# Two interleaved image streams, and the last pair's experts in two turns, in a fused early-fusion kernel on one Trainium2 core

## The reference

```python
scores = jnp.einsum('bnd,bmd->bnm', inputs, inputs) / jnp.sqrt(d_k)      # layer 0, attention
_, idx = jax.lax.top_k(weights, k); sel_idx = idx[:, :kk]                # k = 96, kk = 95
processed = jnp.zeros_like(x).at[batch_idx, sel_idx].set(y)              # layer 0, feed-forward
```

## Time and profile before

| | us |
|---|---|
| median of 3 runs | 513.05 (510.72 to 514.03) |
| the profiled execution | 511.42 |
| its span, first to last instruction | 509.6 |
| TensorE busy | 458.2 (90%) |
| VectorE busy | 344.3 (68%) |
| ScalarE busy | 315.6 (62%) |
| POOL busy | 235.7 (46%) |

### The profile page before, as it was taken

One profiled execution on the slowest core, in us unless ns is written; L12 is line 12 of the kernel. 1 busy time (PEld: TensorE's weight loads), 2 busy tenths in 40 slices (PEclk: granted clock), 3 DMA queues, 4 the chain that ended last, 5 costly groups with the idle time before them and its releaser, 6 DMA issues.

```text
span 509.6 us, 14274 instructions
## 1 busy us (share of the span) xinstructions
PE 458.2 (90%) x5771; PEld 360.2 (71%) x5771; DVE 344.3 (68%) x1151; ACT 315.6 (62%) x675; POOL 235.7 (46%) x266
## 2 busy tenths in 40 slices
PE   7887898989998999989998999889998999789985
PEld 3444577777877878767876787777876787667763
DVE  3588779757995599568975799568956795344220
ACT  2337475767767676787666866778568657463322
POOL 3347733674347634653457525772475246620010
PEclk9999999999999899999999999999999899899999
DMA  8350240023101320033002310132003200231000
GB/s 299 107 99 1 49 96 2 2 44 71 23 10 22 65 44 4 2 82 65 3 4 42 64 32 3 23 65 51 10 3 83 45 3 3 42 72 30 3 1 9
DMA packets 13969, 21.38 MB, mean 42 GB/s; under 512 B 5024, under 2 KB 6544, under 8 KB 13776
## 3 DMA queue, kind: packets, MB, share of 16 engines
q1 hardware_dynamic: 13904, 20.47, 17.3%
HBM read 5.07 MB, written 0.79 MB: 11 GB/s over the span
## 4 chain that ended last, share of the span: by engine, by line
PE 40%; DVE 31%; ACT 14%; POOL 8%; issue 6%; DMA 1%; POOLq 0%; ACTq 0%; DVEq 0%
PE bank L1083 30%; PE bank L1116 9%; DVE negm L695 5%; DVE q_sb L630 4%; DVE tb L630 4%; DVE ssq L646 3%; POOL qs L879 2%; DVE on L712 2%; ACT qT L904 2%; POOL q_sb L872 1%; DMA qM<-mT 1%; ACT qs L904 1%; ACT L1036 1%; ACT xf L915 1%; POOL rsA L806 1%
## 5 line engine op out<-in xcount | busy, mean ns | idle before, releaser
L837 POOL TENSOR_TENSOR q_sb<-q_sb,tb 128x1024 f32<-128x1024 f32 x24 | 57.2, 2385 | 94.5 <-DVE tb L630 94.5
L695 DVE TENSOR_REDUCE negm<-bank 128x2 f32<-128x384 f32 (+2 forms) x112 | 68.1, 608 | 39.3 <-PE bank L1083 38.8
L904 ACT ACTIVATE qT<-bank 128x512 fp32r<-128x512 f32 x96 | 52.4, 597 | 42.8 <-PE bank L1116 42.0
L1083 PE MATMUL bank<-kS,qM 128*128 128x224 f32 (+3 forms) x384 | 64.8, 285 | 7.7 <-issue 4.4
L1083 PEld LDWEIGHTS bank<-kS,qM 128*128 128x128 f32 x384 | 55.0, 194 | 21.8 <-issue 8.6
L879 POOL TENSOR_TENSOR qs<-q_sb,qs 128x1024 fp32r<-128x1024 f32 x24 | 56.7, 2362 | 27.9 <-ACT qs L904 27.7
L1083 PE MATMUL bank<-vx,p 128*64 128x65 f32 x1024 | 65.4, 223 | 0.0
L1036 ACT ACTIVATE p<-bank 128x512 f32<-128x512 f32 x96 | 54.7, 592 | 12.6 <-PE bank L1083 12.3
L1083 PEld LDWEIGHTS bank<-vx,p 128*64 128x64 f32 x1024 | 57.3, 138 | 0.0
L1083 PE MATMUL bank<-qT,kh 128*128 128x512 f32 (+1 forms) x128 | 51.7, 445 | 2.2 <-ACT p L1036 1.2
L1116 PE MATMUL bank<-ident_r,qs 128*128 128x128 f32 x384 | 44.8, 258 | 3.8 <-POOL qs L879 2.7
(11 more groups left out here) (177 smaller groups left out, 1025.4 us busy)
## 6 DMA issues: line engine op xcount, KB each, us to landing
qM<-qT SPq DMA_DIRECT2D x48, 256.0 KB, 3.2
qM<-qM SPq DMA_DIRECT2D x1, 1280.0 KB, 9.3
wts<-weights SPq DMA_DIRECT2D x1, 1059.0 KB, 5.9
p<-masks SPq DMA_DIRECT2D x1, 960.0 KB, 9.8
h<-txt SPq DMA_DIRECT2D x1, 672.0 KB, 7.1
img<-images SPq DMA_DIRECT2D x8, 72.0 KB, 2.2
q_sb<-wqkv SPq DMA_DIRECT2D x1, 576.0 KB, 8.0
p<-experts SPq DMA_DIRECT2D x1, 512.0 KB, 10.3
```

The source lines that it names most:

```text
L695: ve.tensor_reduce(dst, src, AX_X, ALU.max, negate=True).then_inc(s_vec, 1)
L837: return gp.tensor_tensor(a, a, b[:, :, ::-1], ALU.add)
L904: return ac.activation(dst, src, ACT.Copy)
L1083: return pe.matmul(dst, lhsT, rhs, start=start, stop=stop, skip_group_check=True)
```

## The change

1. **Two image streams.** "A" takes the even pairs, a new stream "O" the odd ones. Each has its own buffers and its own four semaphores. Pair 1's image stage runs in `BANK_S` and does not wait for pair 0's; from pair 2 on all lie in `BANK_A` again, and pair n waits for y of pair n-1.
2. **Tokens by image.** The tiles are transposed in the order 0, 2, 1, so that the 192 tokens of an item lie side by side. s01 is 2 matmuls of 192 columns in place of 8, s2 2 in place of 4, route 2 in place of 8, all but s2 with full output rows.
3. **The last pair's experts in two turns.** D has nine turns. The eighth is pair 7's tiles 0 and 1 and begins after wo1; the ninth is tile 2 alone, after wo2, in the two banks `BANK_Q`, so that h1 does not wait for the activation of h0.
4. **Experts' own storage.** `picks`, `hmT` and `xd` get buffers of their own; E6 and E9 no longer wait for D.
5. **New orders.** All five strings of `MERGE`, and `WARM` with 90 and 29 idle matmuls.

The order of TensorE's last steps is, before: wo1 V6 V7 V8 X4 X5 wo2, then D of pair 7 (xT logits oneT h0 h1 h2 h3 out). After: wo1 V6 V7 D7.xT V8 D7.logits X4 D7.oneT D7.h0 D7.h1 X5 D7.h2 D7.h3 wo2 D7.out, then the ninth turn's eight steps. VectorE does D7's ln before V6, the rest of it after V8; ScalarE does h0 and h1 of D7 before the copy of X5.

At the start TensorE does A0.rows cols tok, A1.rows cols tok, A0.xT1 s01 s2, A1.xT1, A0.ctx, A1.s01 s2 ctx, A0.xT2 route h1a, A1.xT2 route, A0.h1b y, A1.h1a h1b, and rows and cols of pair 2 around A1.y, then B. VectorE does rank1 and rank2 of pair 1 before y of pair 0, and rank3 of pair 1 before h of pair 0. ScalarE does xn1 of pair 1 before the second exponential of pair 0, xn2 and xT2 of pair 1 before h1a of pair 0. Before V0 stand E0, E1, E2 and S3; tok, xT1, s01, s2 and ctx of pair 2 stand ahead of E0.

The diff's core (the strings and the repeated indexing by pair left out):

```diff
-D_PE = ["y0", "y1", "y2", "xT", "logits", "oneT", "h0", "h1", "h2", "h3", "out"]
+D_PE = ["xT", "logits", "oneT", "h0", "h1", "h2", "h3", "out"]
...
+def turn(names, pair, name):
+
+    return pair.half * len(names) + names.index(name) + 1
...
            "A": [("A", x) for x in A_ORDER],
+           "O": [("A", x) for x in A_ORDER],
...
+PAIRS_OF = {"D": range(PAIRS + 1), "A": range(0, PAIRS, 2), "O": range(1, PAIRS, 2)}
...
+        xa, xpad = two("xa", [P, NT, D + 1]), two("xpad", [P, 2, D + 1])
+        xaT, h1T = two("xaT", [P, PT]), two("h1T", [P, 2, PT])
...
-        picks = small[:, 0:PT].rearrange("q (t c) -> q t c", t=NT)
+        picks = sb("picks", [P, NT, P])
-        hmT = early21[:, 0:4 * PT].rearrange("k (c q) -> k c q", c=4)
-        xd = small[:, 2 * PT:2 * PT + NT * D].rearrange("q (t d) -> q t d", t=NT)
+        hmT = sb("hmT", [P, 4, PT])
+        xd = sb("xd", [P, NT, D])
...
+        def d_tiles(p):
+
+            return (0, NT) if p.n < PAIRS - 1 else (0, 2) if p.n < PAIRS else (2, NT)
...
+        def d_bank(p, c=0):
+
+            return bank[BANK_D if p.n < PAIRS else BANK_Q[c % 2]]
+
+        def a_bank(p, name=None):
+
+            if p.n == 0 and name is not None:
+                return dict(s2=BANK_O, h1a=BANK_D, h1b=BANK_O, y=BANK_E[0])[name]
+            return BANK_S if p.n == 1 else BANK_A
...
-                    if n == 6:
-                        ac.wait_ge(d_pe, p.n * len(D_PE))
+                    if n in (6, 9) and p.n > 0:
+                        ac.wait_ge(o_pe, p.n * NV)
...
             def a_rows(p):
-                if p.n == 0:
+                if p.n < 2:
                     pe.wait_ge(ld_first, 16)
                 else:
-                    pe.wait_ge(a_vec, p.n * len(A_VEC))
+                    pe.wait_ge(a_vec[p.par], p.half * len(A_VEC))
+                if p.n > 2:
+                    pe.wait_ge(a_vec[1 - p.par], turn(A_VEC, Pair(0, p.n - 1), "y"))
...
-                    transposes(bA, [src[:, t, 0:D] for t in range(NT)], ident, a_pe)
+                    transposes(bank[a_bank(p)], [src[p.par][:, t, 0:D] for t in (0, 2, 1)], ident, a_pe[p.par])
...
                 for b in range(2):
-                    c0, c1 = cols(b)
-                    halves(bA[:, T * b:T * b + P], xaT[:, c0], xaT[:, c0], True, True)
-                    ins = halves(bA[:, T * b + P:T * b + T], xaT[:, c0], xaT[:, c1], True, True)
-                ins.then_inc(a_pe, 1)
+                    ins = mm(bank[a_bank(p)][:, image(b)], xaT[p.par][:, own(b)], xaT[p.par][:, image(b)], True, True)
+                ins.then_inc(a_pe[p.par], 1)
...
-                    pe.wait_ge(d_act, after(D_ACT, p, ["oneT", "h0", "h1", "h2"][c]))
+                    pe.wait_ge(d_act, after(D_ACT, p, ["oneT", "h0", "h1", "h2"][max(0, c - 1) if p.n == PAIRS else c]))
```

More of the change, by code:

```diff
@@ L407, in a_rows @@
                 if p.n + 2 < PAIRS:
-                    sp.wait_ge(a_pe, after(A_PE, p, "rows"))
+                    sp.wait_ge(a_pe[p.par], turn(A_PE, p, "rows"))
                     image(p.n + 2)
@@ L556, in _, with rt @@
             halves = [(slice(0, P), 0, 0, 0), (slice(0, P), 1, 1, 0), (slice(0, 64), 0, 2, 1), (slice(64, P), 1, 2, 1)]
-            before = cs("before").rearrange("q (k s) -> q k s", k=2)
-            rt = bA[:, 0:2 * T].rearrange("q (b t) -> q b t", b=2)
+            seen = cs("before").rearrange("q (k s) -> q k s", k=2)
+            before = [seen[:, :, HALF:HALF + T], seen[:, :, 0:T]]
+            def rt(p):
+                return bA(p)[:, 0:2 * T].rearrange("q (b t) -> q b t", b=2)
             def a_rank1(p):
-                ve.wait_ge(a_pe, after(A_PE, p, "route"))
-                if p.n == 0:
+                ve.wait_ge(a_pe[p.par], turn(A_PE, p, "route"))
+                if p.n < 2:
@@ L576, in a_rank2 @@
                                                   ALU.is_equal, ALU.mult)
-                ins.then_inc(a_vec, 1)
+                ins.then_inc(a_vec[p.par], 1)
             def a_rank3(p):
-                ve.wait_ge(a_vec, after(A_VEC, p, "equal"))
+                ve.wait_ge(a_vec[p.par], turn(A_VEC, p, "equal"))
                 for q, b, t, k in halves:
-                    ins = ve.scalar_tensor_tensor(eq[q, t, :], rt[q, b, :], wcol[q, t:t + 1], eq[q, t, :],
-                                                  ALU.is_gt, ALU.add, accum_out=rank[q, t:t + 1])
@@ L594, in a_y @@
[L594 to L596 removed]
+                ve.tensor_tensor(yA[p.par], bank[a_bank(p, "y")][:, 0:NT * D].rearrange("q (t d) -> q t d", t=NT),
+                                 wt("b2").unsqueeze(1).broadcast_to([P, NT, D]), ALU.add).then_inc(a_vec[p.par], 1)
+                ve.wait_ge(a_vec[p.par], turn(A_VEC, p, "y"))
@@ L604, in b_ln @@
+                ve.tensor_tensor(h0[:, p.n, :, :], hx[p.par][:, :, :], yA[p.par], ALU.add).then_inc(a_vec[p.par], 1)
             def b_ln(p):
-                ve.wait_ge(a_vec, after(A_VEC, p, "h"))
+                ve.wait_ge(a_vec[p.par], turn(A_VEC, p, "h"))
                 sums(h0[:, p.n, :, :], sumsB, b_vec)
@@ L743, in d_pick @@
                 wait_apart(ve, d_vec, after(D_VEC, p, "top"))
-                for t in range(NT):
+                for t in range(lo, hi):
                     ins = ve.max_index(ix[:, t, :], top[:, t, :], lg[:, t, :])
@@ L929, in d_xn @@
                 ac.wait_ge(d_pool, after(D_POOL, p, "shift"))
-                normalise(xd, hC, rsD, nmD, d_act)
+                for t in range(*d_tiles(p)):
+                    ins = ac.activation(xd[:, t, :], hC[:, t, :], ACT.Identity, scale=rsD[:, t:t + 1], bias=nmD[:, t:t + 1])
+                ins.then_inc(d_act, 1)
             def a_do(name, dst, src, func=ACT.Copy, **kw):
                 def f(p):
-                    if p.n == 0 and name[0] == "h1a":
+                    if p.n < 2 and name == "h1a":
                         ac.wait_ge(ld_w, 16)
-                    ac.wait_ge(a_pe, after(A_PE, p, name[0]))
-                    ac.activation(dst, src if src is not None else bank[a_bank(p, name[0])][:, 0:dst.shape[1]], func,
-                                  **kw).then_inc(a_act, 1)
+                    ac.wait_ge(a_pe[p.par], turn(A_PE, p, name))
+                    b = bank[a_bank(p, name if name in ("s2", "h1a", "h1b") else None)]
+                    ac.activation(dst[p.par], b[src[0], 0:src[1]], func, **kw).then_inc(a_act[p.par], 1)
                 return f
             def a_h1(c):
-                return a_do(["h1a", "h1b"][c:c + 1], h1T[:, c, :], None, ACT.Gelu_apprx_tanh,
+                return a_do(["h1a", "h1b"][c], [h[:, c, :] for h in h1T], (slice(0, P), PT), ACT.Gelu_apprx_tanh,
                             bias=wt("b1")[:, c:c + 1])
@@ L1148, in a_xt, with image, own @@
-                return f
-            def cols(b):
-                return slice(P * b, P * b + P), slice(2 * P + HALF * b, 2 * P + HALF * b + HALF)
+                    wait_apart(pe, a_act[p.par], turn(A_ACT, p, wait))
+                    transposes(bank[a_bank(p)], [src[p.par][:, t, 0:D] for t in (0, 2, 1)], ident, a_pe[p.par])
+                return f
+            def image(b):
+                return slice(T * b, T * b + T)
+            def own(b):
+                return slice(2 * P * b, 2 * P * b + P)
@@ L1173, in a_s2 @@
-                ins.then_inc(a_pe, 1)
+                for b in range(2):
+                    q = slice(64 * b, 64 * b + 64)
+                    ins = mm(dst[q, 0:T], xaT[p.par][:, P + 64 * b:P + 64 * b + 64], xaT[p.par][:, image(b)], True, True)
+                ins.then_inc(a_pe[p.par], 1)
             def a_ctx(p):
-                pe.wait_ge(a_act, after(A_ACT, p, "p2"))
-                pe.wait_ge(a_vec, after(A_VEC, p, "pad"))
+                pe.wait_ge(a_act[p.par], turn(A_ACT, p, "p2"))
@@ L1190, in a_route @@
+                ins.then_inc(a_pe[p.par], 1)
             def a_route(p):
-                pe.wait_ge(a_act, after(A_ACT, p, "xT2"))
-                if p.n == 0:
+                pe.wait_ge(a_act[p.par], turn(A_ACT, p, "xT2"))
+                if p.n < 2:
                     pe.wait_ge(ld_w, 16)
                 for b in range(2):
-                    c0, c1 = cols(b)
-                    halves(bA[:, T * b:T * b + P], wt("wr"), xfT[:, c0], True, True)
-                    ins = halves(bA[:, T * b + P:T * b + T], wt("wr"), xfT[:, c1], True, True)
@@ L1279, in f @@
                             pe.wait_ge(set_mask, 1)
+                            pe.wait_ge(a_vec[1], turn(A_VEC, Pair(0, 1), "y"))
                         if p.n < 2:
@@ L1405, in d_xt @@
                 pe.wait_ge(d_pool, after(D_POOL, p, "lo"))
-                transposes(bD[:, :].bitcast(F32R), tiles(xds), ident_r[:, :], d_pe)
+                lo, hi = d_tiles(p)
+                transposes(d_bank(p)[:, P * lo:P * hi].bitcast(F32R), tiles(xds)[lo:hi], ident_r[:, :], d_pe)
             def d_logits(p):
                 pe.wait_ge(d_act, after(D_ACT, p, "xT"))
-                for t in range(NT):
```

(3 more changed lines are left out.)

375 lines of the change are left out of this document (191 added, 184 removed), and 78 rows, old and new, of tables (MERGE, WARM).

## The result

The changed kernel takes 522.49 us, the median of 4 runs (520.52 to 524.27), against 513.54 (510.72 to 515.46) of the kernel before: a ratio of 1.018 (1.013 to 1.022), 9 us slower. I had forecast 504.8. The profiled execution took 524.27 us, its span 522.4.

A forecast was written before the change was run, and what follows sets the result against it. Middle close to full on TensorE, time to be had at the ends; -1.8 - 1.5 - 3.3 - 0.4 = -7.0 us gives 504.4 from 511.42, or 506.0 beside other runs; forecast 504.8, range 500 to 508 (chance 0.50).

The forecast's parts named there:

- Part 1: Start, image stages of pairs 0 and 1 side by side: -1.8 us up to V0, and -1.5 from pair 2's steps.
- +4.4 for pair 0's own stage: Pair 0's image stage ends 4.4 us later, behind pair 1's steps on ScalarE and VectorE; bounds 2.4 to 6.
- -6.2 for the way from pair 0's h to V0: V0 comes 6.2 us sooner after pair 0's start: 3.6 left at E0, another 2.6 from there to V0.
- Rival C: No gain at the ends, 510 us: pair 0's start costs 6, +2 left at V0, tail gives 1.5; chance 0.17.
- -1.5 for pair 2's steps moved ahead of V0: Pair 2's transposes, scores and context leave an 89% busy TensorE stretch: -1.5 us, bounds 0 and -2.1.
- Part 2: Tokens by image, in scores, route and second scores: fewer instructions, same column time, 0 us; bound 1.1 us a pair.
- rival A: TensorE time goes by instructions, so tokens by image save 1.1 us in each of pairs 2 to 7: 498 us; chance 0.17.
- Part 3: Last pair's experts in two turns: tail 8.3 us shorter, second turn begins 4.9 later, net -3.3 us; bounds -8.3 and -1.5.
- The sign of 16 us from wo2's end to the end: Check in the tail: 16 us from the end of wo2 to the end of the span.
- Part 4: Experts' own storage: E6 and E9 no longer wait for the previous experts' output, -0.4 us; bounds 0 and -1.5.
- B: Slower, 517 us: experts' and image steps ahead of attention steps hold it 1.8 us in each of seven periods; chance 0.08.
- D: The clock: with fewer fillers the new tail falls to 1.2 GHz and its 2.5 us of matmuls double, 507 us; chance 0.08.

The follow-up runs named there:

- E9: Not a run but a step of the kernel, which in the changed kernel no longer waits for the previous experts' output; no run has this name.
- experiment 1: Also spelled image_dma_first: the changed kernel, but the DMA queue sends the images of pairs 2 and 3 ahead of the mask rows; 514.07 us, ratio 1.0015 to before.
- image_first_by_tile: The changed kernel with tokens by tile and the images sent ahead of the masks in the DMA queue; 514.57 us, ratio 1.003 to before.
- tail_again: Old orders and tokens by tile, with the two-turn tail, experts' own storage and second image buffers, measured a second time; 508.44 us, ratio 0.990 to before.
- storage_alone: The changed code with tokens by tile, old orders and idle matmuls, pair 7's experts in one turn; 512.81 us, ratio 1.000 to before.
- by_image_alone: The kernel before with tokens by image and nothing else changed; 517.86 us, ratio 1.006 to before.

## Why the prediction was wrong, step by step

By the ratios, in us: the image behind the masks +8.3 (experiment 1); the new orders of start and middle, with that mended, +6.5 (image_first_by_tile against tail_again); the two-turn tail -5.0 (tail_again against storage_alone, with tokens by image -3.1 and, shifted, -3.5); storage 0; tokens by image in these orders about -1, within the error. The sum is 9, as it must be, since each step is measured against the next; each carries an error of about 2 us. My terms for the same steps were 0, -3.3 (-1.8 and -1.5), -3.3, -0.4 and 0. So two steps miss: the image by 8.3 us, and the new orders by some 10.

**Part 1, the start, is the step that failed.** It followed VectorE, ScalarE, POOL and TensorE and left the DMA queue out. The sum had the rows and cols of pair 2 moved around A1.y as free. Their input comes by a DMA that stands behind the masks in its own queue, as it did before. Moving its reader from 66.8 us to 36.1, where TensorE first stood ready for it, put that wait on the path; the DMA queue's string was in the diff.

Of the two terms, +4.4 for pair 0's own stage measured 6.7 (33.59 for the last add). The order behind it was as described:

```profile
28.98 0.29 DVE L592 CUSTOM_DVE_ANT_0 eq<-bank,fst 128x128 f32<-128x128 f32 x1
...
31.27 0.36 DVE L617 TENSOR_TENSOR xa<-bank,wts 128x192 f32<-128x192 f32 x1
...
33.59 0.36 DVE L626 TENSOR_TENSOR h<-hx,xa 128x192 f32<-128x192 f32 x1
```

The rest I had not counted: VectorE and POOL hold each other up. POOL's power for pair 1 took 1.99 us instead of 0.85, under VectorE's split of the weights, and ScalarE stood behind it with pair 1's normalising, ahead of pair 0's second exponential:

```profile
13.02 1.35 DVE L509 TENSOR_TENSOR wq_lo<-q_sb,wq_hi 128x1152 fp32r<-128x1152 f32 x1
13.10 1.99 POOL L839 TENSOR_TENSOR rsA<-rsA,minus_half 128x3 f32<-128x3 f32 x1
```

-6.2 for the way from pair 0's h to V0 was real but too large: it takes 45.8 us before, 45.6 with the late image, and with the image in time 40.7 (image_dma_first) and 41.5 (image_first_by_tile), so -4.3 to -5.1; by V0's first matmul, the mark of the sum, -3.8 to -4.6. Up to S0's maximum 2.2 to 2.7 us were won, of the 3.8 forecast. There the sum has a slip: it put the maximum at 55.2, where S0's matmuls would begin, and not at their end, 57.22 - 2.1 + 0.7 = 55.8. With the fault out V0 lies 2 to 3 us later than before, not 1.8 sooner: 6.5 lost and some 4.7 won. Rival C had this half right.

-1.5 for pair 2's steps moved ahead of V0 did not come. From V0 to hC of pair 0 the profiles have 40.9 us before, 42.7 in image_first_by_tile and 44.7 in image_dma_first.

The two profiles behind the 6.5 us of the new orders (image_first_by_tile and tail_again) lie 3.6 us apart at hC of pair 0, another 1.1 at that of pair 6, and 2.6 more from there to the end, where the first has 6.8 us of half clock around 455 us and the second 3.4. The run-out was no term of my sum; which step in it costs the time is open.

**Part 2, tokens by image: 0.** Right in its own terms: s01 of pair 1 takes 0.92 us in four instructions where sixteen took 0.89.

```profile
17.84 0.92 PE L1122 MATMUL bank<-xaT 128*128 128x192 f32 x4
```

The periods are equal too, so rival A fell. But the change has another price, 1.4 to 3.6 us in four comparisons with the old orders and none seen in the new: fewer instructions move the fetches. No row that I read could have priced it.

**Part 3, the tail: -3.3.** The mechanism was right and nearly the size. From V8 of pair 7 to wo2 the kernel before took 3.4 us and the changed one 6.8, +3.4 for the +3.5 of the text; the second turn begins 9.4 us after V8, by my numbers 9.5, and its chain takes 12.5 us, by mine 12.8:

```profile
505.08 0.60 PE L1155 MATMUL bank<-fst,on 128*128 128x128 f32 x4
...
507.31 1.15 PE L1122 MATMUL bank<-wts,oT 128*64 128x64 f32 x32
509.68 0.29 DVE L792 SCALAR_TENSOR_TENSOR o_sb<-bank,hC 128x128 f32<-128x128 f32 x1 [6.96 <-PE bank L1122]
509.88 0.21 DVE L748 TENSOR_TENSOR hC<-bank,h 128x64 f32<-128x64 f32 x1
```

From V8 to the end it is 21.9 us for 25.7, and 21.9 for 25.8 in tail_again against storage_alone: -3.8 and -3.9. The -5.0, -3.1 and -3.5 of the ratios, each give or take 2 us or more, agree with it. The sign of 16 us from wo2's end to the end did not fit my own terms, which make 14.3; it took 13.9.

**Part 4: -0.4** measured 0.0, within 0.3%. The middle, taken as 0, was that within 3 us: from hC of pair 0 to that of pair 6 the profiles have 329.8 us before, 332.0 after, 327.1 in image_dma_first and 329.1 in image_first_by_tile. My 53.5 us a period was read between convenient marks; by hC it is 55.0.

**The rivals.** B, slower by 1.8 us handed on in each of seven periods, had the sign and the chance of 0.08, but not the mechanism: the periods are 0.4 us longer and not 1.8, and the largest single loss begins at one late image. D looked for the half clock in the tail, where it came only at 520.8 us, behind the last matmul (the 0.94 of the last window). It cost time at the start and between the pairs.

**The clock's share.** Over 291 executions of these kernels, each against its own kernel's mean, 0.01 of mean granted clock goes with 3.3 us (correlation -0.89; for 31 executions of the kernel before alone 3.6 us and -0.94). The changed kernel's mean is 0.968 and that of before 0.986, so by that rate, an estimate, some 6 of the 9 us come with the clock. I take it for no separate cause: the first fall, at 39.5 us, follows the 3.5 us of waiting and goes with the mended DMA order. For the later falls that is argued and not shown. A stall of TensorE can cost more than its length: 3.5 us of waiting for the image went with a loss of 8.

## What to carry to other kernels

When steps are moved in orders written out by hand, follow every queue, the DMA queue's too, and for each moved step ask where its input is sent and what stands ahead of that, even where that order has not changed. Try the repair of a fault before judging the change that carries it, and move idle matmuls on purpose, since they go with the step to which they are tied. When two kernels have equal stages and unequal times, look for a short DMA that lands late, and at what held its engine.

## What the runs showed of the hardware

- TensorE's instructions come by DMA, in packets of 16 KB on the same 16 engines as the data, 0.9 to 1.5 us each in the kernel before. An 8 KB DMA that is spread over all engines landed 1.2 to 1.5 us later beside such a packet in pairs 0 and 1 of by_image_alone, and with it came whoever waited for its last piece. Adding 56 matmuls at one place moved the later fetches; here that was worth 3.4 us in 513, give or take 2.3.
- VectorE and POOL slow each other in small instructions beside large ones. xpad of pair 2 (two instructions on 64 columns) took 2.58 us beside a POOL product of 2.39, 0.64 at the start of the kernel:

```profile
56.44 2.58 DVE L559 TENSOR_SCALAR xpad<-h,mvA,rsA 64x64 f32<-64x64 f32 x2
```

```profile
56.57 2.39 POOL L870 TENSOR_TENSOR q_sb<-q_sb,tb 128x1024 f32<-128x1024 f32 x1
```

  The Trainium skill (SBUF — State Buffer, section "SBUF: two separate sides") calls the port pair that the two engines share an exclusive lock: the one that starts first has it for its whole instruction, and the other waits. On VectorE's side it says so only of instructions in a two-port mode or with two inputs in SBUF. The trace fits it: the second xpad instruction ends at 59.02 us, with the POOL product (58.96) and not before it.
- The clock's state at the start differs between executions, and idle matmuls cost twice as much when it is low: the 8 ahead of tok of pair 1 took 1.90 us in the profile of the changed kernel and 3.59 in that of image_dma_first, where tok began 1.5 us later. The first record of the full clock begins at 5.4 us in the one trace and at 13.1 in the other. Ahead of it the window view prints 1.00 all the same, so there the durations have to be read.
